# An LSTM and a GRU in one kernel: the LSTM's input product by seven block products for two steps

## The reference, cut to what matters

```python
def _L0_cond_ref(x, h0, Wx, Wh, b):          # LSTM, h0 = cond
    xW = jnp.einsum('ntd,dg->ntg', x, Wx) + b
    def step(carry, xw_t):
        prev_h, prev_c = carry
        a = xw_t + prev_h @ Wh               # 4 gates of 512
        i, f, o = sigmoid(a[:, :H]), sigmoid(a[:, H:2*H]), sigmoid(a[:, 2*H:3*H])
        g = jnp.tanh(a[:, 3*H:])
        next_c = f * prev_c + i * g
        next_h = o * jnp.tanh(next_c)
        ...
def _L1_cond_ref(video, seq, ...):           # GRU, video = cond
    def step(h, xs):
        z = jax.nn.sigmoid(xzt + h @ U_z + vz)
        r = jax.nn.sigmoid(xrt + h @ U_r + vr)
        hh = jnp.tanh(xht + r * h @ U + vh)
        h_new = (1.0 - z) * h + z * hh
        ...
x = x + _L0_cond_ref(x, cond_1024, ...)
x = x + _L1_cond_ref(cond_1024, x, ...)
```

## Time and profile before

| | us |
|---|---|
| median of 3 runs (1229.92 to 1232.26) | 1230.14 |
| the profiled execution | 1231.91 |
| its span, first to last instruction | 1230.1 |
| TensorE busy | 1201.3 |
| VectorE busy | 872.3 |
| ScalarE busy | 445.0 |
| POOL busy | 277.7 |

### The profile page before, as it was taken

The page is one execution under the profiler, slowest core; times in us unless marked ns, Lnnn a source line. Parts: engine busy times, 40 slices in busy tenths (PEclk is TensorE's granted clock), DMA queues, the critical chain, the costliest instruction groups (busy, mean ns, idle before and its releaser), DMA issues.

```text
span 1230.1 us, 68313 instructions
## 1 busy us (share of the span) xinstructions
PE 1201.3 (98%) x31174; PEld 831.7 (68%) x31174; DVE 872.3 (71%) x2681; ACT 445.0 (36%) x1078; POOL 277.7 (23%) x520
## 2 busy tenths in 40 slices
PE   5889999999999999999999999999999999999997
PEld 1467676676676766766767667667676676676765
DVE  2768877777777777777777777777777777777765
ACT  5555233333333333333333333333333333333332
POOL 3100222222222222222222221222222222222221
PEclk9899999999999999999999999999999999999999
DMA  9900100111110011110011111011111001110001
GB/s 307 324 8 9 21 16 9 21 21 21 21 21 8 16 21 20 21 21 12 13 21 21 21 21 19 6 21 21 21 21 21 10 14 21 21 21 12 12 4 29
DMA packets 142066, 39.51 MB, mean 32 GB/s; under 512 B 135825, under 2 KB 136081, under 8 KB 140753
## 3 DMA queue, kind: packets, MB, share of 16 engines
q1 hardware_dynamic: 140080, 34.49, 12.3%
q0 software_dynamic: 640, 0.53, 0.2%
q10 hardware_dynamic: 1056, 0.13, 0.1%
HBM read 26.74 MB, written 8.39 MB: 29 GB/s over the span
## 4 chain that ended last, share of the span: by engine, by line
PE 94%; SPq 3%; DVE 1%; DMA 1%; ACT 1%; issue 0%; DVEq 0%; ACTq 0%
PE ps_l L795 51%; PE ps_g L795 38%; PE ps_g L804 3%; SPq L241 2%; DMA o_area<-in_L_cond_C_dram 1%; PE ps_l L804 1%; SPq L245 1%; ACT o_area L354 0%; DVE u L549 0%; DVE zr L552 0%; SPq L252 0%; SPq L250 0%; PE ps_c L804 0%; ACT zr L468 0%; DVE rgT L730 0%
## 5 line engine op out<-in xcount | busy, mean ns | idle before, releaser
L795 PE MATMUL ps_l<-wx,x2T 128*32 128x512 f16 x6020 | 348.7, 379 | 0.0
L795 PE MATMUL ps_l<-wh,h2T 128*32 128x512 f16 x5952 | 344.5, 379 | 0.0
L795 PEld LDWEIGHTS ps_l<-wx,x2T 128*32 128x32 f16 x6020 | 181.5, 97 | 117.9
L795 PE MATMUL ps_g<-w,y2T 128*32 128x384 f16 x5760 | 256.6, 326 | 0.0
L795 PEld LDWEIGHTS ps_l<-wh,h2T 128*32 128x32 f16 x5952 | 173.2, 97 | 116.7
L795 PEld LDWEIGHTS ps_g<-w,y2T 128*32 128x32 f16 x5760 | 175.4, 97 | 71.2
L328 POOL TENSOR_TENSOR yT<-xT,hT 128x128 f32<-128x128 f32 x128 | 61.7, 482 | 582.4 <-DVE hT L679 582.4
L795 PE MATMUL ps_g<-u,g2T 128*32 128x256 f16 x5760 | 179.8, 273 | 1.0 <-ACT g2T L496 1.0
L795 PEld LDWEIGHTS ps_g<-u,g2T 128*32 128x32 f16 x5760 | 160.2, 97 | 11.2 <-issue 1.4
L552 DVE SCALAR_TENSOR_TENSOR zr<-ps_g,sc,term 128x256 f32<-128x256 f32 x128 | 61.9, 484 | 102.6 <-PE ps_g L795 92.8
L312 POOL TENSOR_TENSOR o_area<-yT,gT 128x128 f32<-128x128 f32 x127 | 58.2, 458 | 297.3 <-DVE gT L778 297.3
(11 more groups left out here) (103 smaller groups left out, 1112.8 us busy)
## 6 DMA issues: line engine op xcount, KB each, us to landing
x_nat<-in_x_dram SPq DMA_DIRECT2D x126, 64.0 KB, 2.6
out_dram<-o_area SPq DMA_DIRECT2D x124, 64.0 KB, 2.1
wh<-in_L_cond_Wx_dram SPq DMA_DIRECT2D x4, 1024.0 KB, 11.1
w<-in_L_cond_Wh_dram SPq DMA_DIRECT2D x3, 1024.0 KB, 18.9
u<-in_L_cond_Wh_dram SPq DMA_DIRECT2D x1, 1024.0 KB, 24.6
stage<-in_L_cond_W_z_dram SPq DMA_DIRECT2D x1, 1024.0 KB, 8.5
stage<-in_L_cond_W_r_dram SPq DMA_DIRECT2D x1, 1024.0 KB, 8.2
stage<-in_L_cond_W_dram SPq DMA_DIRECT2D x1, 1024.0 KB, 10.4
```

The costliest lines, as they stand in the source:

```text
L795: mm = nc.tensor.matmul(bank[B * j:B * j + B, c0:c1].rearrange("p (n c) -> p n c", c=B), still(a, k), moving(b, k, j), start=opens and (a, ...
```

## The change

**Seven products for two steps.** From step FW = 28, the inputs' product of an even step u and the next, u + 1, is done as one 2 x 2 block product: the two steps are two rows of blocks, x's 512 inputs two halves, wx's 2048 columns two halves (of 256 columns in each of the four partition groups). Winograd's form of it has 7 block products in place of 8, with four sums of blocks of x (s1 to s4) and four of wx (t1 to t4). `seventh` does one: 3 passes x 2 chunks x 4 matmuls = 24 matmuls of 256 columns, into half a bank. Those of u and u + 1 are spread over the D of steps u - 3 (half of T4's), u - 2 (the rest of T4's, b11's, T1's into `ps_c`), u - 1 (T2's, b21's, b22's) and u (T3's). Partial results that two outputs share leave PSUM: VectorE's `first_out`, `fifth_out`, `sixth_out`, `seventh_out` scale 128 x 256 out of a bank half, add the bias or an earlier one, and write `pre`, which the gates' sums use in place of term0. TensorE waits for `evicted` ahead of the next use of these halves: in an odd step ahead of A, for the seventh out.

**The blocks' sums.** wx is loaded again into `stage` in step 9 (SP waits for all splits of W and U first). POOL makes t1, t3, t2, t4 in steps 11 to 14 (`make_t`, two subtractions of 128 x 1024 each), ScalarE their high parts and VectorE their low parts, in quarters of 128 x 512, one or two in a step from 12 to 23. For each group of four steps POOL makes s1 to s4 (4 x 128 x 128 f32) and ScalarE and VectorE split them in one instruction each (128 x 512).

**Moved.** For groups from NG_W = 7 on: `largest` to q = 2, `turn` and `bound` to q = 3 of two groups ahead, `lstm_scales` to q = 0, x's high part behind the candidate in q = 0, its low part to q = 1. On VectorE `lstm_scales`, x's low part, `largest` and (in all groups) `turn_out` now stand between the gates' sums and ig_fc; `turn_out` and its store come in q = 3 instead of q = 1 of the group behind. The squares' product of step 4 moves from behind A to behind D.

```diff
@@ DVE: the outs, and the gates' sums
+            def first_out(u):
+                evict(1, u, pre[:, u % NL, H1], ps_l[(u + 1) % NL][:, H2], bias0(H1))
+            def fifth_out(u):
+                evict(2, u, pre[:, (u + 1) % NL, H2], ps_fifth[:, H1], bias0(H2))
+            def sixth_out(u):
+                dve.wait_ge(evicted, 2 * (u - FW) + 2)
+                evict(3, u, pre[:, u % NL, H2], ps_l[(u + 1) % NL][:, H2], pre[:, (u + 1) % NL, H2])
+            def seventh_out(u):
+                evict(4, u, pre[:, (u + 1) % NL, H1], ps_l[(u + 1) % NL][:, H2], bias0(H1))
...
+                    if t >= FW:
+                        dve.wait_ge(evicted, 2 * (t - FW) + 3 if t % 2 == 0 else 2 * (t - FW) + 2)
...
+                if len(T_LOW.get(t, ())) > 1:
+                    t_low(T_LOW[t][0])
+                if q == 0 and NG_W <= group + 1 < NG:
+                    lstm_scales(1 - r, group + 1)
+                if q == 1 and NG_W <= group + 1 < NG:
+                    dve.wait_ge(x_hi, group + 1)
+                    lo_part(x2T[:, 1 - r, LO, :], xT[:, 1 - r, :], a_x(1 - r), x2T[:, 1 - r, HI, :]).then_inc(x_lo, 1)
+                if q == 2 and NG_W <= group + 2 < NG:
+                    dve.wait_ge(x_in[r], 16 * J * (i + 2))
+                    largest(r)
+                if q == 3 and group >= 1 and t < T:
+                    dve.wait_ge(out_done[1 - r], 16 * J * ((group - 1) // 2 + 1))
+                    turn_out(1 - r, group - 1)
...
+                if FW <= t < T and q % 2 == 0:
+                    seventh_out(t)
...
+                    if FW <= t + 2 < T and q % 2 == 0:
+                        first_out(t + 2)
+                    if FW <= t + 1 < T and q % 2 == 1:
+                        sixth_out(t + 1)
...
+                    if FW <= t + 2 < T and q % 2 == 0:
+                        fifth_out(t + 2)
@@ PE: ahead of A
+                    if t >= FW and q % 2 == 1:
+                        pe.wait_ge(evicted, 2 * (t - FW) + 2)
@@ PE: squares, from behind A to behind D
-                if t == T_WU_SCALE:
-                    pe.wait_ge(w1_squares, GG)
-                    pe.wait_ge(u1_squares, GG)
-                    squares(2 * K, 2 * GG)
@@ PE: D
-                if FL - 1 <= t < T - 1:
+                if FL - 1 <= t < FW - 1:
...
+                if q % 2 == 0:
+                    if FW <= t < T:
+                        pe.wait_ge(evicted, 2 * (t - FW) + 3)
+                        seventh(ps_l[(t + 1) % NL], 1, s_of(r, 3, q // 2), t_of(N_T3), False).then_inc(seven_ps, 1)
+                    if FW <= t + 2 < T:
+                        u, v = t + 2, t + 3
+                        ru, qu = u // Q % 2, u % Q
+                        if qu == 0:
+                            pe.wait_ge(xs_lo, u // Q - NG_W + 1)
+                        seventh(ps_l[v % NL], 0, a_of(ru, qu + 1, 1), t_of(N_T4), False, FOURTH)
+                        seventh(ps_l[v % NL], 1, a_of(ru, qu, 0), b_of(0, 0), False).then_inc(seven_ps, 1)
+                        if u > FW:
+                            pe.wait_ge(evicted, 2 * (u - FW) - 2)
+                        seventh(ps_fifth, 0, s_of(ru, 1, qu // 2), t_of(N_T1), True).then_inc(seven_ps, 1)
+                elif FW <= t + 1 < T:
+                    u, v = t + 1, t + 2
+                    ru, qu = u // Q % 2, u % Q
+                    pe.wait_ge(evicted, 2 * (u - FW) + 1)
+                    seventh(ps_l[v % NL], 1, s_of(ru, 2, qu // 2), t_of(N_T2), False).then_inc(seven_ps, 1)
+                    pe.wait_ge(ifo_sum, u - NL + 1)
+                    seventh(ps_l[u % NL], 0, a_of(ru, qu, 1), b_of(1, 0), True)
+                    seventh(ps_l[u % NL], 1, s_of(ru, 4, qu // 2), b_of(1, 1), False)
...
```

More of the change, by code:

```diff
@@ L273, in tick @@
                     load(t + 2 * Q, r)
-                if t >= 2 * Q + 1 and t % Q == (1 if t < T else 0):
-                    store(Q * (group - 2), r, group - 2)
+                if t == T_AGAIN:
+                    sp.wait_ge(cand_ps, F - 1)
+                    sp.wait_ge(w1_split, HALVES * GG)
+                    sp.wait_ge(u1_split, HALVES * GG)
+                    for k in range(K):
+                        sp.dma_start(wx_again[k], wx[P * k:P * k + P, :]).then_inc(again_in, 16)
+                if q == Q - 1 and group >= 1:
+                    store(Q * (group - 1), 1 - r, group - 1)
             ticks(tick)
@@ L304, in _ @@
                 pool.sem_inc(out_done[r], 16 * J)
+            pool_made = [0]
             def add_out(s, m, group):
@@ L337, in tick @@
                                             ).then_inc(y_lo, 1)
+                if t == T_MADE:
+                    pool.wait_ge(again_in, 16 * K)
+                    make_t(t1, b12, b11)
+                if t == T_MADE + 1:
+                    make_t(t3, b22, b12)
+                if t == T_MADE + 2:
+                    make_t(t2, b22, t1)
+                if t == T_MADE + 3:
+                    make_t(t4, b21, t2)
+                if q == Q - 1 and NG_W <= group + 2 < NG:
+                    make_s(r, group + 2)
                 if t == T - 1:
@@ L746, in tick @@
                 after_keep(t)
-                if q == 0 and 0 < group < NG - 1:
+                if q == 0 and 0 < group < NG_W - 1:
                     if t >= Q:
@@ L760, in tick @@
                         gru_scales(1 - r, group + 1)
-                if q == 3 and (group + 2 < NG):
+                if q == 3 and group + 2 < NG_W:
                     dve.wait_ge(x_in[r], 16 * J * (i + 2))
@@ L850, in gate_as_given, with seventh, a_of, s_of @@
                 return mm
+            FOURTH = 3
+            halves = [(a, b, k) for a, b in PASSES for k in range(K // 2)]
+            def seventh(bank, half, operand, weights, opens, first=0, last=len(halves)):
+                for a, b, k in halves[first:last]:
+                    for j in range(J):
+                        mm = nc.tensor.matmul(bank[rows(j), 2 * P * half:2 * P * half + 2 * P].rearrange("p (n c) -> p n c", c=B),
+                                              operand(a, k),
+                                              weights(b, k).rearrange("p (n j c) -> p j n c", j=J, c=B)[:, j],
+                                              start=opens and (a, b, k) == halves[0], stop=(a, b, k) == halves[-1],
+                                              skip_group_check=True)
+                return mm
+            def a_of(r, q, half):
+                return lambda a, k: x2T[:, r, a, P * q + B * (2 * half + k):P * q + B * (2 * half + k) + B]
+            def s_of(r, n, m):
+                c = P * (n - 1) + P // 2 * m
+                return lambda a, k: xs2[:, r, a, c + B * k:c + B * k + B]
+            def b_of(half, columns):
+                return lambda b, k: wx2[:, b, 2 * half + k, N2 * columns:N2 * columns + N2]
+            def t_of(n):
+                return lambda b, k: t_parts[n][:, b, k, :]
             pe.wait_ge(zeroed, 3)
@@ new lines, in tick @@
+                if q % 2 == 1 and FW <= t + 3 < T:
+                    u, v = t + 3, t + 4
+                    ru, qu = u // Q % 2, u % Q
+                    if u == FW:
+                        pe.wait_ge(t_split, 4 * QUARTERS)
+                    if qu == 0:
+                        pe.wait_ge(x_lo, u // Q)
+                    pe.wait_ge(ifo_sum, v - NL + 1)
+                    seventh(ps_l[v % NL], 0, a_of(ru, qu + 1, 1), t_of(N_T4), True, 0, FOURTH)
+                if q == 0 and 0 < group < NG_W - 1:
@@ L954, in tick @@
                     bound(1 - r, group + 1)
+                if q == 3 and NG_W <= group + 2 < NG:
+                    bound(r, group + 2)
                 if t >= T - 1:
+                    pe.wait_ge(ifo_sum, T - NL + 1)
                     go_on(7)
```

130 lines of the change are left out of this document (115 added, 15 removed).

## The result

The changed kernel takes 1216.28 us (median of 4 runs, 1216.0 to 1218.1) beside 1230.66 for the kernel before (4 runs): ratio 0.9882, 95% interval 0.987 to 0.9895. It is 14.4 us faster; I had forecast 30 (1200, from 1230.14), and the high end of my range, 1209, was 21. The profiled execution is 1216.41 with a span of 1214.6, against 1231.91 and 1230.1, so its gain is 15.5.

The account below looks back on a forecast made before the run. TensorE, busy 98% of the span, bounds the kernel. 1231.91 - 30.5 (columns) + 2.0 (A's wait) + 1.95 (end) - 4.0 (squares) + 0.4 (weights) = 1201.8, less 1.8 to the median: 1200.0; range 1196 to 1209.

Parts of the forecast that it names:

- Making the weights: Steps 9 to 23, loading, summing and splitting the new weights: a late zr sum costs 0.4 us, bounds 0 to 5.
- The squares: Step 4: moving the squares' product behind D removes TensorE's stand and the slow stretch after it, 4.0 us off, bounds 2 to 4.3.
- Columns: TensorE from step 28: seven 256-column products replace two of 512, 0.61 us less a pair, 30.5 off over 50 pairs.
- Rival 3: TensorE's matmuls: a fixed cost each counts after all, at 38 ns instead of 27 the run takes 1290 us; chance 0.02.
- The link D to E: Between C and E: D's 2.28 us still covers the chain of 2.22 with 0.06 left; cost taken as 0.
- Rival 1: In D: the chain from zr sum to E outlasts D, 0.05 to 0.1 us a step, 1204 to 1210; chance 0.20.
- Four sums out of the banks: VectorE: four PSUM sums of 0.484 us a pair, 0.97 a step, fit in its waits at 88% busy; cost nothing.
- Rival 2: VectorE, between the new sums and the zr sum: it becomes the bound, slower than before, about 1234 us; chance 0.05.
- A new wait with a price: Odd steps: A waits for the seventh out of the even step before, 0.04 us a pair, 2.0 in all, bounds 0 to 5.
- The end: Last steps, 125 to 127: work pulled forward leaves less cover, so TensorE idles; 1.95 us more together.
- Rival 4: Steps 4 to 8: the squares' stand moves to another product and its gain doesn't come, 1204 us; chance 0.08.

Follow-up runs that it names:

- POOL's extra operations: Kernel before with two extra, unused POOL operations of 128 x 1024 in each of six steps (subtractions, memsets or multiplications by a constant): 1234.86 us, a single execution.
- The squares alone: Kernel before with only the squares' product of step 4 moved from behind A to behind D: 1228.23 us against 1230.96, ratio 0.9977.

## Why the prediction was wrong, point by point

- **The step that failed is "Making the weights"**: taken at 0.4, bounded at 5, shown 11.0 in the profiles. 1216.28 less 11 is 1205; the range would have held that. POOL's duration was inside the bounds (2.385, between 0.46 and 3.7), and its results came in time. Wrong was the overlap: the reading that work on an engine with free time is free for the others. I asked whether POOL would be late; the question was who stands while it runs. The bound of 5 took in only late results. What the runs showed instead is VectorE's instructions held to the end of POOL's subtractions, 14.3 us for 2.3, and the 11.0 us gone as soon as POOL's columns were.
- The trace of before had the sign. Its timeline around 151 us:

```profile
151.03 0.74 DVE L549 SCALAR_TENSOR_TENSOR x2T<-xT,sc,x2T 128x512 f16<-128x512 f32 x1
151.06 1.00 POOL L336 TENSOR_TENSOR y2T<-y_scaled,y2T 128x128 f16<-128x128 f32 x1 [0.41 <-ACT y2T L479]
```

  POOL's low part of y takes 0.43 to 0.44 in 90 steps and 0.97 to 1.01 in 30, one of them here, where it starts 0.03 behind an instruction of VectorE of 0.74 with two SBUF operands. Two durations of one shape in one profile, with the neighbour as the difference, are the sign of it. The Trainium skill says it outright (SBUF — State Buffer, "SBUF: two separate sides"): VectorE and GpSimd have one pair of ports in common, "an **exclusive lock**, not a bandwidth split", kept for the whole instruction, for which an instruction of VectorE with two SBUF inputs and one of GpSimd that reads SBUF compete. The runs agree for two operands on both sides (1.6 to 2.4 us for 0.29). They disagree in that POOL's TENSOR_SCALAR, which reads SBUF for 2.75 us, held neither. The same section also lets an instruction of VectorE in a two-port mode compete; that would cover the small TENSOR_SCALAR beside the memset (1.11 and 2.17), but no run here shows in which mode it ran.
- *The squares*: step 4 lost 4.03, as worked out, and the clock was 1.00. But 1.7 of it was the clock, which the profiled execution had lost and the one with POOL's extra operations had not. I took the 1.8 between that execution and the median off the sum as well, so most of the 1.7 us was probably counted twice, and the median should have been forecast at 1201.5 to 1202. The squares alone speak for it, with 2.7 in the medians; no execution at the median was traced.
- *Columns*: 24 matmuls at 0.65 to 0.66, a pair at 17.67, 0.56 less than 18.23 with A's wait in it (forecast 0.57). Over 50 pairs that is 0.5 us. Rival 3 is refuted: a fixed cost for each matmul that adds to a pair doesn't show.
- *The link D to E*: D gives 2.29 and E follows at once in the steady steps. The margin of 0.06 held, but it no longer covers a disturbance: step 41 above. Rival 1 is refuted as a steady state; step 41 shows its tail.
- *Four sums out of the banks*: VectorE 30.2 in 35.25 (forecast 31.0 in 35.2), still waiting 0.68 for C (0.76 before). A sum that only scales and adds a bias out of `ps_c` takes 0.44. Rival 2 is refuted.
- *A new wait with a price*: the seventh out of the step shown above runs to 696.89, and A starts 0.05 later, at 696.94, as worked out:

```profile
696.41 0.48 DVE L676 SCALAR_TENSOR_TENSOR stage<-ps_l,sc,term 128x256 f32<-128x256 f32 x1
```

  E starts at 696.24 and takes 0.67 in the step before (687.43 to 688.10), so A could have come at 696.91. It waits 0.03 (forecast 0.04), which is in the pair's 0.56 above.
- *The end*: step 126 stands 1.38 in E plus the tail of D, 1.56 from start to start (forecast 1.57), against the earlier trace rows:

```profile
1190.71 0.83 PE L1049 MATMUL ps_l<-stage 128*32 128x256 f16 x24
1192.92 0.85 PE L986 MATMUL ps_g<-u,rg2T 128*32 128x128 f16 x48 [1.38 <-DVE rg2T L670]
```

- *Missing from the sum*: the long steps, 2.85 in this profile. Nothing in the trace of before shows them, and I can't say that I could have priced them.
- Rival 4 (the squares' gain doesn't come) is refuted.
- *A slip in the range*: the squares' gain gone and A's wait at its bound give 1200.0 + 4.0 + 3.0 = 1207, and not 1209. The other way to 1209, 0.09 a step in D, holds, so the range stays as it was.

## What to carry to other kernels

Before giving an idle GpSimd work on SBUF, look in the trace for one shape of VectorE or GpSimd that has two durations, and see what ran beside the long one: that is the sign that the two engines hold each other. In this kernel the price was paid for the length of GpSimd's instruction by the chain through VectorE, 2.4 us at a time. The same work was cheaper on VectorE itself, in pieces of 0.68 us placed in its waits. And when a profiled execution lies above the median, find the rows that make it so before an edit's gain is read from them: a gain in just those rows is not in the median.

## What the runs showed of the hardware

- VectorE's 128 x 128 instructions with two SBUF operands, 0.29 us, last up to 2.34 beside POOL's subtraction of 128 x 1024 (2.385 us), and end within 0.15 us of its end. Sums with one operand in PSUM keep their 0.34.
- POOL's memset of 128 x 1024 (0.92 us) holds a TENSOR_SCALAR of 128 x 2 to its end (1.11 and 2.17), and so does the subtraction (1.66 and 1.74); POOL's TENSOR_SCALAR of 128 x 1024 (2.75 us) holds neither this one nor zc.
- A subtraction on POOL takes 2385 ns for 1024 columns. In rows of eight pieces of 128 columns a piece takes 509 ns on average: 54 of 64 take 0.45 to 0.51, the longest 0.91, beside VectorE's work.
- The clock after the same stand of 2.3 us in step 4 was 0.66 in one execution and 1.00 in another, 1.67 us apart.
- TensorE pauses with no releaser, idle for 0.32 us in step 84 of the changed kernel, in steps that issue 276 matmuls in 8.84 us; no step of the kernel before, with 240 in 9.11, is longer than 9.14 from step 10 on. The cause is open.
